# Change to a fused attention and mixture-of-experts kernel: expert weights by one-input products, second one-hots in columns over 32 steps, one late re-gather a step

## The chip, the core and the metric

One NeuronCore of a Trainium2 chip. The metric is the time of one execution in microseconds, as the device measures it; of several runs the median. Engines: TensorE (PE; its weight loads are PEld), VectorE (DVE), ScalarE (ACT), GpSimd (POOL) and SyncE (SP), which issues direct DMAs. Gathers and scatters by index are issued by GpSimd.

## The reference, cut to what matters

```python
# x, ctx: (64, 128, 256) f32
q = layernorm(x)
score = softmax(einsum('bci,bcj->bij', ctx, q) / 16, axis=0)    # over the 64 batches
x = x + einsum('bci,bij->bcj', ctx, score)
h = layernorm(x)                                                # 8192 tokens of 256
logits = h @ router_w.T                                         # 8 experts
top2, idx = top_k(logits, 2);  probs = softmax(top2)
y = sum over the 2 experts: probs * (gelu(h @ w1[e].T + b1[e]) @ w2[e].T + b2[e])
out = x + y
```

The softmax runs over the batches, so its maximum and its sum need all scores before any output. Each token goes to two of eight experts, so the tokens are sorted by expert.

## The kernel before

The work runs in stages, each a loop written once per engine; semaphores order the engines against each other.

1. Scores and their maximum over the batches, then the scores again with exponentials and their sum, both in 32 pairs of batches. The expert weights are transposed and split in two f16 parts beside the second pass.
2. `attend`, 32 pairs, software-pipelined: TensorE transposes ctx (L591), multiplies (L617), transposes the normalised rows (L599) and makes router logits (L607). GpSimd normalises the probabilities of the first 320 columns (L480) and works out the norm's scale (L452 to L457); VectorE normalises the other columns (L817), adds the residual (L781), takes statistics (L798, L813) and picks the top two. Eight weights a row (the softmax of the top two, spread over the experts) are written by L803, one product of two tensors for both batches of the pair. SyncE stores each pair's rows to a table in memory, 520 floats a token: the row so far, the normalised row in two f16 parts, the eight weights. Within `attend` the first 8 pairs and the tail are unrolled with fixed addresses, and 24 pairs run in a hardware loop.
3. Routing. Each token has a place in a list sorted by expert, for each of two rounds: in the first round it goes to the lower-numbered of its two experts, in the second to the other. `list_tokens` turns places into a list by TensorE: for each of the 64 batches a one-hot of the token's lane (128) is the weight and a one-hot of its tile (76), times a mark that holds the token's number, is the moving operand; 64 matmuls accumulate in one bank. VectorE makes the one-hots in `one_hots(rnd, q)`, 16 batches at a time, with the batch as the innermost, contiguous index, so TensorE reads them at a stride of 64 f16. `indices` turns the bank into gather and scatter indices.
4. Experts. Per round 38 groups of 256 tokens, 76 in all, in steps of one group, each step in the same order on each engine. In step i GpSimd gathers group i and then stores group i-4; TensorE does the first matmul of group i-3 (L664), the transposes of group i-2 (L675) and the second matmul of group i-4 (L687); ScalarE does the gelu (L1038) and copies the transposes (L1046); VectorE splits the activations of group i-3 in two f16 parts (L930, L932), adds its bias (L919), and adds the second matmul of group i-4 to the rows (L946). The first round reads the first table and writes the second; the second round reads the second table and writes the output.

At the boundary, groups 38 to 41 (the first four of round two) are gathered from the first table ahead of time, for the normalised rows alone; their running sums aren't known yet. In step 42 GpSimd waits for all stores of round one and then gathers these groups once more from the second table (L509, `late_loads`), and VectorE waits for that (`x_late_in`) before bias and sum of such a group. Each engine works through its instructions in order, so a wait holds all that is behind it.

The order: `one_hots(1, q)` stands in steps 0 to 3 behind the group's work on VectorE; `list_tokens(1)` at the end of step 36 on TensorE; `indices(1)` in step 37 on VectorE. Steps 0 to 5 are unrolled, 6 to 35 are a loop of six a turn, 36 to 47 are unrolled again.

Of the kernel before, what the change touches and what calls it, by code (L numbers as in the profile page):

```python
# [30 lines left out]
ALU = mybir.AluOpType  # L31
# [3 lines left out]
P = 128  # L35
BATCH, ROWS, DIM = 64, 128, 256
EXPERTS, HID = 8, 512
# [5 lines left out]
GROUPS = TOKENS // GROUP + EXPERTS - 2  # L43
TILES = GROUPS * SUB
# [6 lines left out]
PR = 2 * DIM  # L51
# [10 lines left out]
L_TR, L_G1, L_G2 = 2, 3, 4  # L62
# [74 lines left out]
def xattn_ffn(nc, x, ctx, router_w, w1, b1, w2, b2, out):  # L137
# [7 lines left out]
    with ExitStack() as stack:  # L145
# [31 lines left out]
        iota16 = smax[:, 0, 192:256].bitcast(F16)  # L177
# [3 lines left out]
        mark = smax[:, 0, 288:320].bitcast(F16)  # L181
# [18 lines left out]
        def slot(b, first, n):  # L200

            return slots[:, bass.ds(b * ROW + first, n)]

        def slot2(b, first, n):

            return slots3[:, bass.ds(b, 2), first:first + n]
# [143 lines left out]
        ALL = ROUNDS * GROUPS  # L350
        LIST_BANK = (4, 1)
        LIST_STEP = GROUPS // LANES * LANES

        def is_step(i, k, step):

# [2 lines left out]
        def is_late(g):  # L358

            return isinstance(g, int) and GROUPS <= g < GROUPS + L_G2  # L360

        def late_loads(step):

            first = step - L_G2 + (step > GROUPS + L_G2)
            return [g for g in range(first, step - L_G2 + 2) if is_late(g) and step >= GROUPS + L_G2]

        L_CTX = 2
        L_MAX = 3
# [163 lines left out]
        def _(pe):  # L532
# [104 lines left out]

            def list_tokens(rnd):

                tiles = tile_hot.rearrange("p (n b) -> p n b", b=BATCH)  # L640
                lanes = lane_hot.rearrange("p (l b) -> p l b", b=BATCH)
                w = BATCH // 4
                for b in range(BATCH):
                    q = b // w
                    if b % w == 0:
                        pe.wait_ge(r_lane, 4 * rnd + q + 1)
                        pe.wait_ge(r_tiles, 4 * rnd + q + 1)
                    mm = pe.matmul(psum[:, LIST_BANK[rnd], 0:TILES], lanes[:, :, b], tiles[:, :, b], start=(b == 0), stop=(b == BATCH - 1))
                mm.then_inc(r_list, 1)

            list_tokens(0)
# [45 lines left out]
        def _(dve):  # L697
# [63 lines left out]
            def attend(i, k, n):  # L761
# [38 lines left out]
                if live(i, k, L_P, PAIRS):  # L800
                    m, r2 = i + k - L_P, (k - L_P) % 2
                    dve.wait_ge(a_inv, m + 1)
                    dve.tensor_tensor(slot2(m * 2, PR, EXPERTS), exps[:, r2, :, 0, :], inv[:, r2, :].unsqueeze(2).to_broadcast([P, 2, EXPERTS]),  # L803
                                      ALU.mult).then_inc(a_comb, 1)
                if live(i, k, L_LG, PAIRS):
                    m, r2 = i + k - L_LG, (k - L_LG) % 2
                    dve.wait_ge(a_topi, m + 1)
# [67 lines left out]
            def one_hots(rnd, q):  # L875
# [8 lines left out]
                dve.wait_ge(r_ones, 4 * rnd + q + 1)  # L884
                dve.tensor_tensor(hot_b, one, mark[:, b].unsqueeze(1).to_broadcast([P, TILES, BATCH // 4]), ALU.mult).then_inc(r_tiles, 1)

            def indices(rnd):

                dve.wait_ge(r_list, rnd + 1)
                own = slice(rnd * TILES, (rnd + 1) * TILES)  # L890
                chain(dve.tensor_scalar(listed, psum[:, LIST_BANK[rnd], 0:TILES].bitcast(I32), 13, None, ALU.arith_shift_right))
                chain(dve.tensor_scalar(index_in[:, own], listed, float(-LISTED_ZERO), 0.0, ALU.add, ALU.max),
                      dve.tensor_scalar(empty, listed, 0.0, float(LISTED_ZERO + SKIPPED), ALU.is_equal, ALU.mult))
                dve.scalar_tensor_tensor(index_out[:, own], listed, float(-LISTED_ZERO), empty, ALU.add, ALU.add).then_inc(r_index, 1)
# [28 lines left out]
            def group(i, k, n, rnd):  # L923
# [23 lines left out]
                                                        rows[:, X2:X2 + DIM], ALU.mult, ALU.add)  # L947
                    last.then_inc(x_sum, 1)

                if isinstance(i, int) and i + k < 4:  # L950
                    one_hots(1, i + k)
                if is_step(i, k, LIST_STEP + 1):
                    indices(1)
            expert_steps(dve, group)
# [112 lines left out]
```

## Time and profile before

| | us |
|---|---|
| median of 3 runs | 801.28 (800.5 to 802.1) |
| profiled execution | 800.47 |
| its span on the core | 798.6 |

| engine | busy us | share of the span |
|---|---|---|
| TensorE matmul | 728.4 | 91% |
| TensorE weight load | 632.7 | 79% |
| VectorE | 620.0 | 78% |
| GpSimd | 538.7 | 67% |
| ScalarE | 384.9 | 48% |

The mean granted clock of TensorE was 0.949 of 2.4 GHz. A matmul's record lasts longer than its share of the engine, since they are pipelined; the spacing of starts is what it costs. A wait for a port or a lock counts as busy time of the instruction that waits, a wait for a semaphore as idle time ahead of it. Timelines give start, duration, engine, line, operation, count, and in brackets idle time before it with what ended it.

### The profile page before, as it was taken

What the parts mean: (1) busy time and instruction counts of PE and PEld (TensorE: products, weight loads), DVE (VectorE), ACT (ScalarE), POOL (GpSimd) and SP (SyncE); (2) the same over time, 40 slices, a digit from 0 to 9 for tenths busy, and PEclk for the clock granted to TensorE, in tenths of its full rate; (3) what the DMA queues carried; (4) which work ended last, traced back from release to release, by engine and by line L of the source; (5) the groups of instructions that cost most, each with busy time, mean ns of one, the idle gap of its engine ahead of it and who ended that gap; (6) DMA issues with size and microseconds to landing.
All of it is one profiled execution on the core that took longest, in us unless ns stands there. A gap on an engine that the chain in (4) does not pass through costs nothing. (4 is left out here: it accounts for less than half of the span.)

```text
span 798.6 us, 22383 instructions
## 1 busy us (share of the span) xinstructions
PE 728.4 (91%) x5819; PEld 632.7 (79%) x5820; DVE 620.0 (78%) x1514; ACT 384.9 (48%) x738; POOL 538.7 (67%) x649
## 2 busy tenths in 40 slices
PE   6999999599999955499999999999979999999995
PEld 4777888487777744399999999998967999999994
DVE  6998999989999988787777777636466777676764
ACT  3554666457777763144444444514433544444441
POOL 5664777678888840647777777754677777777753
PEclk9999999799999965699999999979999999999998
DMA  7887777247788751435555555653354444444440
GB/s 236 252 260 236 237 227 226 90 133 243 259 262 261 252 203 59 113 124 195 169 196 177 190 169 161 188 152 88 103 155 143 141 123 149 120 149 124 145 128 29
DMA packets 81630, 137.09 MB, mean 172 GB/s; under 512 B 9755, under 2 KB 54820, under 8 KB 81456
## 3 DMA queue, kind: packets, MB, share of 16 engines
q0 software_dynamic: 22528, 68.06, 28.1%
q1 hardware_dynamic: 59056, 68.46, 26.9%
q8 instruction: 24, 0.39, 0.2%
q14 instruction: 22, 0.18, 0.1%
HBM read 94.00 MB, written 47.24 MB: 177 GB/s over the span
## 5 line engine op out<-in xcount | busy, mean ns | idle before, releaser
L1038 ACT ACTIVATE work<-psum,b1T 128x256 f32<-128x256 f32 x304 | 127.7, 471 | 252.7 <-PE psum L664 250.1
L664 PE MATMUL psum<-work,w1T_high 128*128 128x256 f16 x1216 | 206.5, 275 | 2.8 <-ACT work L1046 2.8
L687 PE MATMUL psum<-w2T_high,slots 128*128 x1216 | 206.4, 275 | 0.9 <-issue 0.9
L664 PE MATMUL psum<-work,w1T_low 128*128 128x256 f16 x608 | 167.2, 275 | 0.0
L687 PE MATMUL psum<-w2T_low,slots 128*128 x608 | 167.2, 275 | 0.0
L664 PEld LDWEIGHTS psum<-work,w1T_high 128*128 x1216 | 119.9, 99 | 18.0 <-issue 3.3
L545 PE MATMUL psum<-slots,work 128*128 (+1 forms) x512 | 124.8, 392 | 7.0 <-ACT slots L963 5.8
L930 DVE CAST slots<-work 128x512 f16<-128x512 f32 x152 | 66.6, 438 | 81.9 <-ACT work L1038 80.5
L687 PEld LDWEIGHTS psum<-w2T_high,slots 128*128 128x128 f16 x1216 | 116.8, 99 | 14.5 <-issue 1.4
L518 POOL DMA_INDIRECT slots<-rows_first,slots x84 | 86.3, 1027 | 55.7 <-issue 53.5
L545 PEld LDWEIGHTS psum<-slots,work 128*128 128x128 f32 x512 | 93.7, 192 | 33.3 <-issue 17.7
L525 POOL DMA_INDIRECT rows_second<-slots x76 | 81.3, 1070 | 54.1 <-issue 29.7
L932 DVE TENSOR_TENSOR slots<-work,slots 128x512 f16<-128x512 f32 x152 | 106.4, 700 | 5.2
L525 POOL DMA_INDIRECT out_x<-slots x76 | 80.8, 1063 | 41.0 <-issue 34.3
L919 DVE SCALAR_TENSOR_TENSOR slots<-slots 128x256 f32<-128x256 f32 x152 | 67.4, 484 | 41.5 <-issue 28.1
L1046 ACT ACTIVATE work<-psum 128x1024 f16<-128x1024 f16 x76 | 77.8, 1024 | 28.3 <-PE psum L675 28.3
L518 POOL DMA_INDIRECT slots<-rows_second,slots x68 | 68.9, 1013 | 20.7 <-issue 20.7
L946 DVE SCALAR_TENSOR_TENSOR slots<-psum,slots 128x256 f32<-128x256 f32 x152 | 66.6, 479 | 19.0 <-DVE slots L919 11.7
L617 PE MATMUL psum<-slots,work 128*128 (+1 forms) x256 | 64.6, 396 | 4.5 <-DVE slots L817 4.5
L472 POOL TENSOR_TENSOR smax<-slots,smax 128x768 f32<-128x768 f32 x31 | 56.5, 1822 | 17.0 <-ACT slots L970 15.1
L664 PEld LDWEIGHTS psum<-work,w1T_low 128*128 x608 | 60.1, 99 | 7.4
L687 PEld LDWEIGHTS psum<-w2T_low,slots 128*128 128x128 f16 x608 | 60.0, 99 | 7.5
(124 smaller groups left out, 1092.4 us busy)
## 6 DMA issues: line engine op xcount, KB each, us to landing
work<-in_ctx SPq DMA_DIRECT2D x96, 256.0 KB, 3.4
rows_first<-slots SPq DMA_DIRECT2D x32, 520.0 KB, 3.1
slots<-in_x SPq DMA_DIRECT2D x32, 256.0 KB, 3.9
work<-in_L_ffn_w SPq DMA_DIRECT2D x32, 256.0 KB, 3.3
work<-in_x SPq DMA_DIRECT2D x32, 256.0 KB, 3.1
slots<-rows_first,slots POOLq DMA_INDIRECT x84, 3.6
rows_second<-slots POOLq DMA_INDIRECT x76
slots<-rows_second,slots POOLq DMA_INDIRECT x76, 3.6
```

The lines of the kernel that those rows point to most:

```text
L518: pool.indirect_dma_start(row_buf[r * SUB + s], None, source, bass.IndirectOffsetOnAxis(ap=index_in[:, g * SUB + s:g * SUB + s + 1], axis= ...
L525: pool.indirect_dma_start(table[1] if g < GROUPS else out_rows, bass.IndirectOffsetOnAxis(ap=index_out[:, g * SUB + s:g * SUB + s + 1], ax ...
L545: mm = pe.matmul(psum[:, r2, h * DIM:(h + 1) * DIM], ctx_ring[:, place, h * P:(h + 1) * P], slot(b, 0, DIM), start=True, stop=True)
L617: mm = pe.matmul(psum[:, 2 + r, j * DIM:(j + 1) * DIM], a_ctxT[:, 2 * r + j, h * P:(h + 1) * P], slot(m * 2 + j, h * DIM, DIM), start=(h = ...
L664: mm = pe.matmul(h, w1T[pw][:, f, c, bass.ds(e * P, P)], xT[r2][:, (px * HC + c) * GROUP:(px * HC + c + 1) * GROUP], start=(c == 0 and px ...
L687: mm = pe.matmul(y, act16[r2][pa][:, f * GROUP + s * P:f * GROUP + (s + 1) * P], w2T[pw][:, f, bass.ds(e * DIM, DIM)], start=(f == 0 and p ...
L919: last = dve.scalar_tensor_tensor(rows[:, X2:X2 + DIM], b2_all[:, bass.ds(e * DIM, DIM)], rows[:, bass.ds(e + PR, 1)], rows[:, X2:X2 + DIM ...
L930: dve.tensor_copy(act16[r2][0][:, cols], act32[r2][:, cols]).then_inc(x_high, 1)
L932: dve.tensor_tensor(act16[r2][1][:, cols], act32[r2][:, cols], act16[r2][0][:, cols], ALU.subtract).then_inc(x_low, 1)
L946: last = dve.scalar_tensor_tensor(rows[:, X2:X2 + DIM], psum[:, 6 + r2, s * DIM:(s + 1) * DIM], rows[:, bass.ds(e + PR, 1)], rows[:, X2:X2 ...
L1038: last = act.activation(act32[r2][:, f * GROUP:(f + 1) * GROUP], psum[:, 2 + 2 * r2 + f // 2, (f % 2) * GROUP:(f % 2 + 1) * GROUP], ACT.Ge ...
L1046: act.activation(xT[r2], psum[:, 0, :].bitcast(F16), ACT.Copy).then_inc(x_xT, 1)
```

## The change

Three parts. The expert weights of a pair are two `tensor_scalar` products, one a batch, whose scalar is the column `inv` read per partition, in place of one `tensor_tensor` over both. The one-hots of the second round are laid out with the batch outermost, made for two batches at a time in steps 4 to 35 (`LIST_FROM` is 36 - 32 = 4), and `list_tokens(1)` reads them as contiguous blocks behind one wait. `late_loads(step)` gives one group a step: 38 in step 42, 39 in 43, 40 in 44, 41 in 45, where it gave 38 and 39 in step 42, 40 in 43 and 41 in 44.

```diff
--- before.py
+++ after.py
@@ -350,6 +350,7 @@
         ALL = ROUNDS * GROUPS
         LIST_BANK = (4, 1)
         LIST_STEP = GROUPS // LANES * LANES
+        LIST_FROM = LIST_STEP - BATCH // 2
 
         def is_step(i, k, step):
 
@@ -361,8 +362,7 @@
 
         def late_loads(step):
 
-            first = step - L_G2 + (step > GROUPS + L_G2)
-            return [g for g in range(first, step - L_G2 + 2) if is_late(g) and step >= GROUPS + L_G2]
+            return [step - L_G2] if is_late(step - L_G2) else []
 
         L_CTX = 2
         L_MAX = 3
@@ -637,15 +637,18 @@
 
             def list_tokens(rnd):
 
-                tiles = tile_hot.rearrange("p (n b) -> p n b", b=BATCH)
-                lanes = lane_hot.rearrange("p (l b) -> p l b", b=BATCH)
-                w = BATCH // 4
                 for b in range(BATCH):
-                    q = b // w
-                    if b % w == 0:
-                        pe.wait_ge(r_lane, 4 * rnd + q + 1)
-                        pe.wait_ge(r_tiles, 4 * rnd + q + 1)
-                    mm = pe.matmul(psum[:, LIST_BANK[rnd], 0:TILES], lanes[:, :, b], tiles[:, :, b], start=(b == 0), stop=(b == BATCH - 1))
+                    if rnd:
+                        lane, tile = lane_hot[:, b * P:(b + 1) * P], tile_hot[:, b * TILES:(b + 1) * TILES]
+                        if b == 0:
+                            pe.wait_ge(r_lane, 4 + BATCH // 2)
+                            pe.wait_ge(r_tiles, 4 + BATCH // 2)
+                    else:
+                        lane, tile = lane_hot.rearrange("p (l b) -> p l b", b=BATCH)[:, :, b], tile_hot.rearrange("p (n b) -> p n b", b=BATCH)[:, :, b]
+                        if b % 16 == 0:
+                            pe.wait_ge(r_lane, b // 16 + 1)
+                            pe.wait_ge(r_tiles, b // 16 + 1)
+                    mm = pe.matmul(psum[:, LIST_BANK[rnd], 0:TILES], lane, tile, start=(b == 0), stop=(b == BATCH - 1))
                 mm.then_inc(r_list, 1)
 
             list_tokens(0)
@@ -800,8 +803,9 @@
                 if live(i, k, L_P, PAIRS):
                     m, r2 = i + k - L_P, (k - L_P) % 2
                     dve.wait_ge(a_inv, m + 1)
-                    dve.tensor_tensor(slot2(m * 2, PR, EXPERTS), exps[:, r2, :, 0, :], inv[:, r2, :].unsqueeze(2).to_broadcast([P, 2, EXPERTS]),
-                                      ALU.mult).then_inc(a_comb, 1)
+                    for j in range(2):
+                        last = dve.tensor_scalar(slot(m * 2 + j, PR, EXPERTS), exps[:, r2, j, 0, :], inv[:, r2, j:j + 1], None, ALU.mult)
+                    last.then_inc(a_comb, 1)
                 if live(i, k, L_LG, PAIRS):
                     m, r2 = i + k - L_LG, (k - L_LG) % 2
                     dve.wait_ge(a_topi, m + 1)
@@ -884,6 +888,19 @@
                 dve.wait_ge(r_ones, 4 * rnd + q + 1)
                 dve.tensor_tensor(hot_b, one, mark[:, b].unsqueeze(1).to_broadcast([P, TILES, BATCH // 4]), ALU.mult).then_inc(r_tiles, 1)
 
+            def one_hots_of_second(j):
+
+                b = BATCH + j * 2
+                one, two = tile_one[:, bass.ds(j * 2 * TILES, 2 * TILES)], tile_hot[:, bass.ds(j * 2 * TILES, 2 * TILES)]
+                as_tiles, as_lanes = "p (b n) -> p b n", "p (b l) -> p b l"
+                dve.tensor_tensor(one.rearrange(as_tiles, b=2), tile_of[:, bass.ds(b, 2)].unsqueeze(2).to_broadcast([P, 2, TILES]),
+                                  iota16[:, 0:TILES].unsqueeze(1).to_broadcast([P, 2, TILES]), ALU.is_equal).then_inc(r_ones, 1)
+                dve.tensor_tensor(lane_hot[:, bass.ds(j * 2 * P, 2 * P)].rearrange(as_lanes, b=2), lane_of[:, bass.ds(b, 2)].unsqueeze(2).to_broadcast([P, 2, P]),
+                                  iota16.unsqueeze(1).to_broadcast([P, 2, P]), ALU.is_equal).then_inc(r_lane, 1)
+                dve.wait_ge(r_ones, j + 5)
+                dve.tensor_tensor(two.rearrange(as_tiles, b=2), one.rearrange(as_tiles, b=2), mark[:, bass.ds(j * 2, 2)].unsqueeze(2).to_broadcast([P, 2, TILES]),
+                                  ALU.mult).then_inc(r_tiles, 1)
+
             def indices(rnd):
 
                 dve.wait_ge(r_list, rnd + 1)
@@ -947,8 +964,8 @@
                                                         rows[:, X2:X2 + DIM], ALU.mult, ALU.add)
                     last.then_inc(x_sum, 1)
 
-                if isinstance(i, int) and i + k < 4:
-                    one_hots(1, i + k)
+                if rnd == 0 or (isinstance(i, int) and LIST_FROM <= i + k < LIST_STEP):
+                    one_hots_of_second(i + k - LIST_FROM)
                 if is_step(i, k, LIST_STEP + 1):
                     indices(1)
             expert_steps(dve, group)
```

## Rows read from the trace of the kernel before

**Rows 1.** The page's first part: busy us (share) and instructions of each engine.
```profile
PE 728.4 (91%) x5819; PEld 632.7 (79%) x5820; DVE 620.0 (78%) x1514; ACT 384.9 (48%) x738; POOL 538.7 (67%) x649
```
**Rows 2.** Busy time by stretch; the last three columns are clock, DMA share, GB/s.
```profile
core 0: us, PE busy (x) PEld busy (x) DVE busy (x) ACT busy (x) POOL busy (x), PEclk, DMA share, GB/s
230.00:250.00 20.00, 18.57 (x120) 15.80 (x120) 20.00 (x88) 14.18 (x37) 16.57 (x25) 1.00 0.82 265
530.00:536.00 6.00, 6.00 (x39) 6.00 (x38) 0.00 (x0) 0.00 (x0) 2.88 (x3) 0.50 0.72 190
```
**Rows 3.** Timeline of VectorE in the loop of attend.
```profile
237.09 0.88 DVE L803 TENSOR_TENSOR slots<-smax 128x16 f32 x1
237.90 0.16 DVE L808 CAST smax<-topi 128x4 uint32 x1
237.97 0.24 DVE L813 BATCH_NORM_AGGREGATE mv<-stats 128x2 f32<-128x6 f32 x2
238.13 0.52 DVE L817 TENSOR_TENSOR slots<-slots,smax 128x384 f32 x1
```
**Rows 4.** Timeline of GpSimd in the same stretch.
```profile
236.41 1.54 POOL L480 TENSOR_TENSOR slots<-slots,smax 128x640 f32 x1
238.37 0.36 POOL L452 TENSOR_SCALAR veps<-mv 128x2 f32<-128x2 f32 x1 [0.42 <-DVE mv L813]
...
240.39 1.54 POOL L480 TENSOR_TENSOR slots<-slots,smax 128x640 f32 x1
```
**Rows 5.** Timeline of VectorE, two instructions with one input.
```profile
176.61 0.98 DVE L808 CAST smax<-topi 128x4 f32<-128x4 uint32 x1
...
289.68 4.24 DVE L770 TENSOR_SCALAR smax<-smax 128x2 f32<-128x2 f32 x1
```
**Rows 6.** Timeline of GpSimd at the same two places.
```profile
176.01 1.55 POOL L480 TENSOR_TENSOR slots<-slots,smax 128x640 f32<-128x640 f32 x1
...
289.33 4.56 POOL L493 IOTA slots<- 128x4864 f16 x1 [1.88 <-DMA rows_first<-slots]
```
**Rows 7.** Groups by line and form: count, busy us, mean ns, idle before.
```profile
L803 DVE TENSOR_TENSOR slots<-smax 128x16 f32 x24 | 22.5, 936 | 0.0
...
L842 DVE TENSOR_TENSOR slots<-slots,before 64x1024 f16<-64x1024 f16 x1 | 1.2, 1216 | 0.0
```
**Rows 8.** Waits between 400 and 523 us: total, times, longest.
```profile
DVE slots L930 <- ACT work L1038: 18.7, 35, 1.1
```
**Rows 9.** Timeline of TensorE: the second list, and the next transposes.
```profile
526.08 10.68 PE L648 MATMUL psum<-slots 128*128 128x76 f16 x64
540.90 0.61 PE L675 MATMUL psum<-ident,slots 128*128 128x128 f16 x8
```
**Rows 10.** The chain of work that ended last, at the boundary: start, us, what.
```profile
586.09 3.62 DMA slots<-rows_second,slots
...
601.38 4.46 PE psum L687 x24
605.84 2.62 PE psum L664 x24
608.46 0.45 PE psum L675 x8
608.90 2.62 PE psum L687 x24
```
**Rows 11.** Timeline of GpSimd at the boundary.
```profile
575.82 0.95 POOL L509 DMA_INDIRECT slots<-rows_second,slots  x1 [0.30 <-issue]
...
581.91 1.27 POOL L525 DMA_INDIRECT out_x<-slots  x1 [1.22 <-issue]
```
**Rows 12.** Timeline of VectorE at the boundary.
```profile
580.02 0.88 DVE L946 SCALAR_TENSOR_TENSOR slots<-psum,slots 128x256 f32<-128x256 f32 x2
...
591.64 0.88 DVE L946 SCALAR_TENSOR_TENSOR slots<-psum,slots 128x256 f32<-128x256 f32 x2
...
600.03 0.88 DVE L946 SCALAR_TENSOR_TENSOR slots<-psum,slots 128x256 f32<-128x256 f32 x2
...
602.34 0.69 DVE L932 TENSOR_TENSOR slots<-work,slots 128x512 f16<-128x512 f32 x1
```

## The prediction

> **What bounds the kernel now.** I read the page's shares first [rows 1]: TensorE is busy 91% of the 798.6 us span, VectorE 78%. An average over unlike stages says little, so next came the busy time by stretch [rows 2] and, for each place that the change touches, the timelines of the engines that meet there. The profiled execution took 800.47 us, its span plus 1.87 around it; the runs' median is 801.28, so what the sum gives is raised by 0.8 for the forecast. Differences under 0.2% (1.6 us) could not be told from no change.
>
> Attention: between 230 and 250 VectorE is busy all of the time and TensorE 18.57 of 20 [rows 2]. A pair of batches takes 3.98 us: the spacing of GpSimd's two products [rows 4]. The reader should see one thing in [rows 3, 4]: L803, 16 elements a partition, lasts 0.88 us and ends at 237.97, just when GpSimd's L480 (236.41 plus 1.54 = 237.95) lets go. In the 24 pairs of the loop it lasts 936 ns on average [rows 7]. It waits for GpSimd; the work is small.
>
> Experts: TensorE bounds. A group costs it 0.45 for transposes and twice 2.62 [rows 10], 5.69 us. Two things break that: the second token list, 64 matmuls in 10.68 us [rows 9], and the boundary of the rounds.
>
> **Part 1, the expert weights (L803).** One two-input product becomes two one-input products, each with a per-partition scalar from SBUF. If these didn't wait, VectorE would have 0.8 us less per pair. Do they wait? The trace has no such instruction, but two near it. The cast L808, one input, lasted 0.98 us at 176.61 [rows 5] and ended at 177.59, with GpSimd's L480 running from 176.01 to 177.56 [rows 6]; this was a pair in which L803 wasn't there yet. The tensor_scalar L770, two elements, lasted 4.24 us at 289.68 and ended at 293.92 [rows 5], with GpSimd's iota L493 from 289.33 to 293.89 [rows 6]. So a cast and a tensor_scalar wait for GpSimd as L803 does. The new instruction is a tensor_scalar of f32 in SBUF; what sets it apart is that its scalar is read from memory. I take it to wait.
>
> The Trainium skill speaks against this edit in the same way (SBUF — State Buffer, Who interferes with whom): copies, casts and tensor_scalars can enter a mode that takes both ports and so contend with GpSimd. The trace agrees with it in the two rows above. The same section says that a one-input instruction outside these modes doesn't contend; that would be rival A.
>
> Then the loop is this. L813 ends, GpSimd starts L452 at 238.37, its L480 ends at 241.93 [rows 4], L803 is let go, L808 and L813 follow, and GpSimd starts again. Everything between L480's end and L813's lies on the cycle. The second product adds one small instruction there: 0.07 us, the distance from L808 to L813 [rows 3]. Over 32 pairs: **+2.3 us** (0 to +3). This is also what VectorE pays where nothing waits.
>
> **Part 2, one-hots in columns, and the list.** Removed: 4 sets of three long instructions in steps 0 to 3. Three sets lay in the time before the first hidden block, where VectorE has nothing else, and the fourth after the first group's casts; TensorE waited there for gathers and for ScalarE's copy of the transposes, not for VectorE. Worth nothing. GpSimd's first gathers lose a neighbour, but the first of them is issued before these one-hots. Zero, at most -1.
>
> Moved to steps 4 to 35: three instructions of 152, 256 and 152 elements a step, each with an operand repeated along its innermost dimension. L842, f16 with such an operand, took 1216 ns for 1024 elements [rows 7], 1.19 ns each. 560 elements come to 0.66, and three starts at 0.07 [rows 3] make 0.87 us a step, as an upper end; with the fixed part of L842 left out, about 0.8. What covers it: between 400 and 523 VectorE waited 18.7 us for ScalarE's activations [rows 8], over 123/5.69 = 21.6 steps, 0.87 us a step. The cover is as large as the cost and not larger. Some lag can also be absorbed once: the last one-hots are due only behind TensorE's second block of the step after, so about one block of 2.62 us [rows 10]. So I cost it at **+0.3**. If loop addresses and extra waits add 0.2 us a step, 32 steps give 6.4, less 2.6: up to +4 (rival C). What queues behind these instructions is the next group's casts, and behind them TensorE's second matmul a step later.
>
> The list itself: before, weights and moving columns are read at a stride of 128 bytes; 10.68/64 = 167 ns a pair [rows 9]. After, both are contiguous. The nearest rows are the transposes L675, also a 128x128 f16 weight load and a matmul each, contiguous: 8 in 0.45 us, 56 ns each [rows 10]. 64 of them: 3.6 us. **-7.1**. Behind the list the granted clock was 0.50, of 2.4 GHz, which is the lower of its levels: it stood at that from 530 to 536 [rows 2] after sparse matmuls, and the following L664 block ran from 526.08 + 10.68 = 536.76 to 540.90 [rows 9], 4.14 us where 2.62 is the rule [rows 10]. A list of 3.6 us ends at 529.7, ahead of the first stretch that is at 0.50, so I take the clock to stay up: **-1.5**. Together -8.6. The other end: at half clock twice 56 ns, 7.2 us, and no clock gain: -3.5.
>
> The Trainium skill (TensorE: Matmul & The Clock Gate, Back-to-back issue gap) gives about 81 ns for a sustained pair of weight load and matmul of 128 columns. By that estimate the list takes 5.2 us and the forecast is 1.6 us higher. The trace shows 56, and the measurement decides.
>
> **Part 3, the late re-gathers.** Groups 38 to 41 must be gathered again from the second table. Before, GpSimd issues 38 and 39 in step 42, 40 in 43, 41 in 44: each but the first one step ahead. After, 38, 39, 40, 41 in steps 42, 43, 44, 45: the step in which VectorE needs them. On GpSimd's queue a re-gather stands behind the store of the group before, and that store waits for VectorE's sum of that group, which itself waited for its re-gather. So they become a chain. Its period can be read off, since before has one such link, from the sum of 38 to the sum of 40. The second half of the sum of 38 ends at 580.90 [rows 12]; store at 581.91 [rows 11]; the re-gather's second half issued at 586.09 lands 3.62 later [rows 10]; bias and sum end at 592.52 [rows 12]. 11.6 us. Before, it carried two groups, since 39 had been issued at 575.82 [rows 11]. After, each group needs one: sums of 39, 40, 41 at 592.5, 604.1, 615.8 on before's clock, where before has the last at 600.03 + 0.88 = 600.9 [rows 12].
>
> Who waits: VectorE works in order, so the casts of group 43 stand behind the sum of 41. Casts and differences end 603.03 - 600.91 = 2.1 us after it [rows 12], so at 617.9. TensorE needs them for its second matmul of group 43, which before started at 608.90 [rows 10]: 9.1 us later. It will have idled long by then, and after the idle at the same boundary such a block took 4.46 instead of 2.62 [rows 10]: 1.8 more. **+10.9** (+9 to +11.5). What is given back: the three gathers after that are issued behind one re-gather each instead of two at first, so the early part of the boundary's stall shrinks, but all of it lies before the new last wait. Afterwards GpSimd needs 4 issues of about 1.25 us [rows 11] in 5.69, so it doesn't fall behind. If a stall of this size were hidden, it would be through slack of VectorE to TensorE, some 3 to 4 us; that is already used in the recurrence.
>
> **Sum:** 800.47 + 2.3 + 0.3 - 8.6 + 10.9 = 805.4; with 0.8 up to the median, 806.2, stated as 806.0.
>
> **The rivals.** *A, the other side: the products don't wait for GpSimd* (27%). For: they read one tensor only. Against: [rows 5, 6]. Then L817, two inputs [rows 3], meets L480 in L803's place, so the 0.8 isn't all gained: GpSimd's own work from L452 to the end of L480 is 3.56 us [rows 4] and TensorE's 18.57 of 20 [rows 2] is 3.70 a pair. The period falls from 3.98 to 3.70, over 24 pairs -7, and the +2.3 goes: 796.7. It decides once the freed time is over 0.2 us a pair. *B, the late chain costs half* (8%), if VectorE's delay were taken up by the order of TensorE's work: 800.5. *C, VectorE becomes the bound of the first round* (10%): 810. *D, the contiguous list is no faster* (5%): the change doesn't do what it says there; 814.6.
>
> **Numbers.** Forecast 50%, at 806, itself 803 to 809. A 795 to 799.5, B 799 to 802. The range 795.5 to 809.5 leaves out the low edge of A, most of C, and D. Faster is nearly all of A and a little of B: 0.30; same, most of B: 0.08; slower, the forecast, C and D: 0.62.
>
> **What would show it.** Part 1: the last product ends with L480, its first lasting some 0.8 us, period 4.05; A shows both at 0.1 and L817 long, period 3.7. Part 2: list under 4 us at clock 1.00, the next L664 block 2.62; VectorE's wait for ScalarE near zero in steps 4 to 35, TensorE without gaps. Part 3: sums of 38 to 41 each 11.6 us apart and TensorE idle before group 43. I am wrong if [rows 5] don't speak for a scalar read from memory, or if that chain is shorter.

## The result, and the profile after

The changed kernel takes **810.17 us** (median of 4 runs, 809.6 to 811.9) where the kernel before took 800.93 on the same chip: ratio 1.0103, 95% interval 1.0086 to 1.0121, slower by 9.2 us (1.0%). Its profiled execution took 810.69 us with a span of 808.8, against 800.47 and 798.6 before.

First the page's first part: busy us, share of the span and instructions of each engine.

```profile
PE 726.9 (90%) x5819; PEld 629.5 (78%) x5820; DVE 635.4 (79%) x1630; ACT 384.9 (48%) x738; POOL 536.2 (66%) x649
```

Against [rows 1] TensorE has the same instructions, VectorE 116 more and 15.4 us more busy time. That says nothing of where 10.2 us of span went. For this, take the start of the same instruction in both profiled executions at a few places and see how the distance changes:

| place | before | after | after is late by | new in this stretch |
|---|---|---|---|---|
| routing's cast behind attention, VectorE | 301.50 | 308.83 | 7.33 | +7.33 |
| second token list, TensorE | 526.08 | 533.35 | 7.27 | -0.06 |
| first transposes behind it | 540.90 | 538.54 | -2.36 | -9.63 |
| sum of group 38, VectorE | 580.02 | 577.62 | -2.40 | -0.04 |
| second block of group 44, TensorE | 614.43 | 624.29 | 9.86 | +12.26 |
| end of the span | 798.6 | 808.8 | 10.2 | +0.3 |

One large gain, two large losses, and nothing in the 225 us of routing and round one. Now each of them in the timelines (start us, duration us, engine, line; brackets: idle before it, and what ended it). Line numbers are those of the changed kernel: its products are L807, its cast into `choice` L812, the list's matmuls L651, the two blocks' matmuls L667 and L690, the transposes L678, the bias L936, the sum L963, the casts L947, the differences L949; the second round's one-hots are L896, L898 and L901. L817 is the norm's statistics, for which GpSimd's L452 waits; L1055 is ScalarE's gelu.

VectorE and then GpSimd, in the loop of attention:

```profile
242.65 1.01 DVE L807 TENSOR_SCALAR slots<-smax 128x8 f32 x2
243.57 0.16 DVE L812 CAST smax<-topi 128x4 uint32 x1
243.64 0.23 DVE L817 BATCH_NORM_AGGREGATE mv<-stats 128x2 f32<-128x6 f32 x2
```

```profile
241.96 1.54 POOL L480 TENSOR_TENSOR slots<-slots,smax 128x640 f32 x1
244.04 0.36 POOL L452 TENSOR_SCALAR veps<-mv 128x2 f32<-128x2 f32 x1 [0.54 <-DVE mv L817]
246.06 1.55 POOL L480 TENSOR_TENSOR slots<-slots,smax 128x640 f32 x1
```

The two products together last 1.01 us and end at 243.66; GpSimd's L480 ended at 241.96 + 1.54 = 243.50. The first waits as the single one did in [rows 3, 4]. Only then comes the second, so GpSimd's L452 starts 0.54 behind its own L480, where it was 0.42, and the pair takes 246.06 - 241.96 = 4.10 us instead of 3.98.

TensorE at the list, and VectorE in a step of round one:

```profile
533.35 2.41 PE L651 MATMUL psum<-slots 128*128 128x76 f16 x64
535.91 0.39 PE L667 MATMUL psum<-work,w1T_high 128*128 128x256 f16 x2
```

```profile
404.81 0.31 DVE L896 TENSOR_TENSOR slots<-slots,smax 128x152 f16 x1
...
405.60 0.42 DVE L947 CAST slots<-work 128x512 f16<-128x512 f32 x1
```

The same 64 pairs of weight load and matmul, 2.41 us in place of 10.68 [rows 9], 38 ns each. The clock isn't what made the old list slow: its pairs started 164 ns apart in the first 3.7 us, at a granted clock of 1.00, and 165 ns apart in the rest, at 0.50. The block behind them runs from 535.91 to the transposes at 538.54, 2.63 us: full clock. The one-hots cost 405.60 - 404.81 = 0.79 us a step. Waits of VectorE between 400 and 523 us (total, times, longest) and the busy time in that stretch (PE, PEld, DVE, ACT, POOL, then clock, DMA share, GB/s):

```profile
DVE slots L947 <- ACT work L1055: 0.7, 4, 0.2
```

```profile
400.00:523.00 123.00, 123.00 (x1212) 111.19 (x1210) 103.19 (x238) 55.93 (x108) 90.45 (x88) 1.00 0.57 180
```

The wait for ScalarE, 18.7 us in [rows 8], is down to 0.7, and TensorE is busy all 123 us, as before. Group by group, its first blocks start 7.27 us later than before from group 1 to group 33, always the same distance: the one-hots went just where the slack was.

The boundary of the rounds. First the chain of work that ended last (start, us, what; L509 is the late re-gather, L525 the store), then TensorE's waits there, with the place in the profile before that the table's fifth row is measured from:

```profile
578.02 0.49 DVE slots L963
...
579.35 0.40 POOL out_x L525
...
580.75 1.00 POOL out_x L525
...
582.05 0.99 POOL slots L509
...
583.35 4.61 DMA slots<-rows_second,slots
...
589.25 0.49 DVE slots L936
...
590.28 0.49 DVE slots L963
...
616.52 4.06 PE psum L690 x24
```

```profile
580.76 0.39 PE L690 MATMUL psum<-w2T_high,slots 128*128 x2 [1.64 <-DVE slots L949]
590.02 1.03 PE L678 MATMUL psum<-ident,slots 128*128 128x128 f16 x8 [3.85 <-DMA slots<-rows_second,slots]
593.02 0.61 PE L690 MATMUL psum<-w2T_high,slots 128*128 x2 [1.96 <-DVE slots L949]
...
614.66 0.62 PE L678 MATMUL psum<-ident,slots 128*128 128x128 f16 x8 [2.61 <-DMA slots<-rows_second,slots]
616.52 0.61 PE L690 MATMUL psum<-w2T_high,slots 128*128 x2 [1.25 <-DVE slots L949]
...
624.29 0.39 PE L690 MATMUL psum<-w2T_high,slots 128*128 x2 [0.46 <-DVE slots L949]
```

```profile
614.43 0.38 PE L687 MATMUL psum<-w2T_high,slots 128*128 x2
```

Read the chain as a circle: sum, two stores, two re-gathers, landing, bias, sum. It goes round three times, from the sum of group 38 to that of 41. VectorE's four sums start at 577.62, 589.88, 601.83 and 613.38, that is 12.3, 12.0 and 11.5 us apart. TensorE now waits twice a turn: for gathered rows, and for L949, the differences that stand behind the late sum on VectorE.

### The profile page after: what moved, and what is told of

It is laid out like the page before. It is cut to its first block and busy times, and to the rows that moved or that the text cites. A ratio compares the mean times of both kernels' runs of the same rounds, so it can differ in the third digit from the quotient of the medians.

```text
span 808.8 us, 22700 instructions
## 1 busy us (share of the span) xinstructions
PE 726.9 (90%) x5819; PEld 629.5 (78%) x5820; DVE 635.4 (79%) x1630; ACT 384.9 (48%) x738; POOL 536.2 (66%) x649
## 5 line engine op out<-in xcount | busy, mean ns | idle before, releaser
L1055 ACT ACTIVATE work<-psum,b1T 128x256 f32<-128x256 f32 x304 | 127.5, 470 | 253.0 <-PE psum L667 250.3
L690 PE MATMUL psum<-w2T_high,slots 128*128 x1216 | 208.6, 277 | 7.2 <-DVE slots L949 7.1
L667 PE MATMUL psum<-work,w1T_high 128*128 128x256 f16 x1216 | 205.2, 274 | 3.0 <-ACT work L1063 2.8
L690 PE MATMUL psum<-w2T_low,slots 128*128 x608 | 168.5, 277 | 0.0
L667 PE MATMUL psum<-work,w1T_low 128*128 128x256 f16 x608 | 166.6, 274 | 0.0
L690 PEld LDWEIGHTS psum<-w2T_high,slots 128*128 128x128 f16 x1216 | 117.4, 99 | 22.2 <-issue 8.4
L667 PEld LDWEIGHTS psum<-work,w1T_high 128*128 x1216 | 119.4, 98 | 18.0 <-issue 3.6
L545 PE MATMUL psum<-slots,work 128*128 (+1 forms) x512 | 125.1, 393 | 7.0 <-ACT slots L980 5.9
L525 POOL DMA_INDIRECT out_x<-slots x76 | 80.3, 1057 | 54.6 <-issue 42.7
L936 DVE SCALAR_TENSOR_TENSOR slots<-slots 128x256 f32<-128x256 f32 x152 | 67.4, 484 | 58.3 <-issue 36.0
L525 POOL DMA_INDIRECT rows_second<-slots x76 | 80.2, 1056 | 46.3 <-issue 29.6
L947 DVE CAST slots<-work 128x512 f16<-128x512 f32 x152 | 67.7, 445 | 54.8 <-ACT work L1055 52.8
L949 DVE TENSOR_TENSOR slots<-work,slots 128x512 f16<-128x512 f32 x152 | 106.5, 701 | 5.2
L963 DVE SCALAR_TENSOR_TENSOR slots<-psum,slots 128x256 f32<-128x256 f32 x152 | 66.6, 479 | 19.8 <-DVE slots L936 14.2
L617 PE MATMUL psum<-slots,work 128*128 (+1 forms) x256 | 66.5, 406 | 4.5 <-DVE slots L821 4.5
L690 PEld LDWEIGHTS psum<-w2T_low,slots 128*128 128x128 f16 x608 | 60.3, 99 | 7.8
L667 PEld LDWEIGHTS psum<-work,w1T_low 128*128 x608 | 59.8, 98 | 7.3
```

What stands on the lines that cost most here:

```text
L525: pool.indirect_dma_start(table[1] if g < GROUPS else out_rows, bass.IndirectOffsetOnAxis(ap=index_out[:, g * SUB + s:g * SUB + s + 1], ax ...
L545: mm = pe.matmul(psum[:, r2, h * DIM:(h + 1) * DIM], ctx_ring[:, place, h * P:(h + 1) * P], slot(b, 0, DIM), start=True, stop=True)
L617: mm = pe.matmul(psum[:, 2 + r, j * DIM:(j + 1) * DIM], a_ctxT[:, 2 * r + j, h * P:(h + 1) * P], slot(m * 2 + j, h * DIM, DIM), start=(h = ...
L667: mm = pe.matmul(h, w1T[pw][:, f, c, bass.ds(e * P, P)], xT[r2][:, (px * HC + c) * GROUP:(px * HC + c + 1) * GROUP], start=(c == 0 and px ...
L690: mm = pe.matmul(y, act16[r2][pa][:, f * GROUP + s * P:f * GROUP + (s + 1) * P], w2T[pw][:, f, bass.ds(e * DIM, DIM)], start=(f == 0 and p ...
L936: last = dve.scalar_tensor_tensor(rows[:, X2:X2 + DIM], b2_all[:, bass.ds(e * DIM, DIM)], rows[:, bass.ds(e + PR, 1)], rows[:, X2:X2 + DIM ...
```

## The experiments

All are the kernel before with one edit, unless said otherwise. Each was timed beside runs of the kernel before on its own chip, whose medians were 801.4, 802.1 and 802.3 us, so the ratios and the differences in us are against those. They tell apart: does each part cost what its term of the sum says, do the parts add, and is the wait of the products really what sets attention's pace.

**One part alone.** The diffs are the three parts of the change. Part 1:

```diff
-dve.tensor_tensor(slot2(m * 2, PR, EXPERTS), exps[:, r2, :, 0, :], inv[...].to_broadcast(...), ALU.mult)
+for j in range(2):
+    last = dve.tensor_scalar(slot(m * 2 + j, PR, EXPERTS), exps[:, r2, j, 0, :], inv[:, r2, j:j + 1], None, ALU.mult)
```

> The kernel before with part 1 alone: two one-input products a pair in place of L803. Theory (the products wait for GpSimd's L480, and the second one adds its start): in the changed kernel the pair's period is 4.10 us against 3.98, so 24 pairs give 3 us and the unrolled ones 1 more: 4 us slower, 805. In the changed kernel's profile attention had lost 7.3 us, of which 3.6 lie in one place at 188 to 203 us where a ctx load took 5.5 us and TensorE's clock fell; if that belongs to the products, this kernel is 7 us slower, 808; if it is a chance of that execution, it is absent here. Rival (they don't wait and the loss is elsewhere): faster, or the same.

Measured: 805.82 us, ratio 1.0053 (1.0032 to 1.0074), +4.4 us. GpSimd's L480 recurs every 4.10 us and, once a turn of the loop, 4.34 (before 3.98 and 4.20); its eighth and its last start are 99.68 us apart, against 96.76 before: +2.9 in 24 pairs. VectorE's row is that of the whole change, its rows moved in time only:

```profile
239.42 1.01 DVE L804 TENSOR_SCALAR slots<-smax 128x8 f32 x2
```

Part 2 is the one-hots in columns and the contiguous list (the diff's `one_hots_of_second` and `list_tokens`):

> The kernel before with part 2 alone: the second round's one-hots in columns over steps 4 to 35, and the contiguous list. Theory: in the changed kernel the first round took 194.18 us from its first L664 block to the list against 194.06, and from the list to the next transposes 5.19 against 14.82, so 9.6 us faster, 791, if the boundary moves as a whole with it. Rival (the boundary is bound by GpSimd, which was given time by the long list): half of it is taken back at the boundary, 796.

Measured: 790.79 us, ratio 0.9868 (0.9851 to 0.9885), -10.6 us. TensorE at the list:

```profile
526.28 2.41 PE L652 MATMUL psum<-slots 128*128 128x76 f16 x64
```

It starts 0.2 us later than before (routing's cast is 0.27 later too), so round one lost nothing, and the next transposes come at 531.40, 9.50 earlier. The other 1.2 us of the profile came at the boundary. The block of group 42, 4.46 us in [rows 10], took 2.79 here: TensorE's granted clock between 590 and 600 was 1.00, where before had 0.83 from 600 to 610. But that isn't part 2's doing. The same block in the chains of two runs told below, which gather late as before: first with the product moved ahead, where the list is the old one, then the whole without part 3, where it is the new one:

```profile
600.15 2.79 PE psum L687 x24
...
597.84 4.46 PE psum L691 x24
```

Either length occurs with either list, so this 1.2 us is a difference between executions, and what part 2 gains by its trace is the 9.50, inside the 9.2 to 11.9 of the runs.

Part 3, one late re-gather per step:

```diff
-first = step - L_G2 + (step > GROUPS + L_G2)
-return [g for g in range(first, step - L_G2 + 2) if is_late(g) and step >= GROUPS + L_G2]
+return [step - L_G2] if is_late(step - L_G2) else []
```

> The kernel before with part 3 alone: one late re-gather a step. Theory (a chain of 11.6 to 12 us from sum to sum): sums of 38 to 41 stand 11.6 to 12 us apart, the second block of group 43 starts about 10 us later, 11 to 12 us slower, 812. Rival (part of the loss in the changed kernel comes of part 2, whose short list leaves GpSimd or VectorE no pause before the boundary): 5 to 8 us slower, 807.

Measured: 815.27 us, ratio 1.0173 (1.0156 to 1.0190), +13.9 us. The sums are 11.9, 11.5 and 12.1 us apart. The chain shows the same circle (lines are one less than the unchanged code's, L508 the re-gather, L524 the store):

```profile
584.02 1.00 POOL out_x L524
...
585.33 0.99 POOL slots L508
...
586.62 4.29 DMA slots<-rows_second,slots
```

The expectation had 11 to 12 us; the median shows 13.9 (12.5 to 15.2), the trace of this run, whose time was the lowest of its four, 12.1 at the boundary. Each part has the sign that the sum gave it, and 4.4 - 10.6 + 13.9 = +7.7 beside the whole's 9.2; the intervals reach about 1.5 us to either side of each part, so this is agreement. The whole without part 3 asks the same from the other side:

> The changed kernel with the late chain taken back (products and one-hots as in the change, the late re-gathers as before). Additive parts: 801.4 + 4.4 - 10.6 = 795.2 us (before x 0.9922), and the late chain then costs 810.2 - 795.2 = 15 us in the company of the other two, against the 13.9 that it cost alone. Rival: the parts share a cost (the list's early end gives the late chain a head start, or a longer attention hides part of it): the late chain then costs clearly less than 13.9 here and this kernel runs at 797 us or more.

Measured: 796.58 us, ratio 0.9922 (0.9901 to 0.9944), -5.7 us where parts 1 and 2 alone sum to -6.2. The late chain in company costs (1.0103 - 0.9922) x 801 = 14.5 us, beside 13.9 alone. The parts add, within these intervals; by the traces they lie in separate stretches.

**Does the kind of product matter?** A single product over both batches, with a constant as its scalar. This leaves out the division by the row's own sum, so it is for the timing alone:

```diff
-dve.tensor_tensor(slot2(m * 2, PR, EXPERTS), exps[:, r2, :, 0, :], inv[...].to_broadcast(...), ALU.mult)
+dve.tensor_scalar(slot2(m * 2, PR, EXPERTS), exps[:, r2, :, 0, :], 0.0078125, None, ALU.mult)
```

> The kernel before with L803 as a single one-input product over both batches, its scalar an instruction constant and not the row's own factor; so the expert weights aren't divided by their own sum, which leaves out that part of the computation. Theory (a one-input product waits for L480 as the two-input one does, whatever its scalar, and the loss of the products is only the second instruction): it lasts about 0.88 us in the loop, the period is 3.98, the time is that of the kernel before, 801. Rival (the products wait only because their scalar is read from memory): it lasts 0.2, and the cast behind it waits 0.65 as in the run with L803 moved; 799.

Measured: 801.27 us, ratio 0.9988 (0.9971 to 1.0005): nothing. VectorE's row, with GpSimd's L480 from 236.56 to 238.10:

```profile
237.25 0.89 DVE L803 TENSOR_SCALAR slots<-smax 128x16 f32 x1
```

It ends at 238.14, with L480 again, and the period is 3.98. A product with one input waits for GpSimd whether its scalar comes from memory or not. What part 1 lost comes of the second product and, it seems, of the memory scalar too. Where GpSimd isn't at work (part 1 alone, then this run):

```profile
284.98 0.35 DVE L804 TENSOR_SCALAR slots<-smax 128x8 f32<-128x8 f32 x2
285.24 0.16 DVE L809 CAST smax<-topi 128x4 f32<-128x4 uint32 x1
...
281.41 0.15 DVE L803 TENSOR_SCALAR slots<-smax 128x16 f32<-128x16 f32 x1
281.48 0.16 DVE L807 CAST smax<-topi 128x4 f32<-128x4 uint32 x1
```

The cast starts 0.26 us behind the pair and 0.07 behind the single product with a constant, 0.13 for each product with a memory scalar in place of 0.07. Two products with constants weren't run, so how much of it each of the two differences makes is not shown.

**Can the wait be avoided?** The product as it was, moved in VectorE's order ahead of `max_index`, where L480 hasn't begun:

```diff
+(L803's product, here)
 for j in range(2):
     last = dve.max_index(topi[:, r2, j, :], ...)
 ...
-(L803's product, from here)
```

> The kernel before with L803 unchanged in kind but moved ahead of max_index, to where GpSimd is in its short steps and L480 hasn't begun. Theory (L803 waits for L480 by its place, and in its absence L817 meets the end of L480): L803 lasts about 0.15 us, L817 gets longer than 0.52, the pair's period falls from 3.98 to 3.6 to 3.7, GpSimd's own work or TensorE's; 24 pairs give 7 us, 794. Rival (the period is set by something else, such as the ctx loads): L803 short, the period stays near 3.98, the same time.

Measured: 799.02 us, ratio 0.9972 (0.9958 to 0.9985), -2.3 us. VectorE's and GpSimd's timelines:

```profile
236.78 0.17 DVE L794 TENSOR_TENSOR slots<-smax 128x16 f32 x1
...
237.81 0.65 DVE L810 CAST smax<-topi 128x4 uint32 x1
...
236.88 1.55 POOL L480 TENSOR_TENSOR slots<-slots,smax 128x640 f32 x1
238.77 0.36 POOL L452 TENSOR_SCALAR veps<-mv 128x2 f32<-128x2 f32 x1 [0.34 <-DVE mv L815]
```

The product is down to 0.17 us, but the cast behind it, 4 elements with one input, now lasts 0.65 and ends at 238.46, L480 at 238.43. The wait has moved to the next instruction that meets L480; only 0.08 us, about what one small instruction takes, left the cycle, and the period is 3.90, not the 3.6 to 3.7 expected. So the cast was moved too, to the end of VectorE's step:

> The kernel before with L803 ahead of max_index and the cast L808 at the end of the pair's work, so that neither stands beside L480. In the run with L803 alone moved, the cast took 0.65 us, again to the end of L480, and the period was 3.90. Theory (the next instruction that can wait does): now only L817 waits, behind L813, so GpSimd is no longer held by VectorE's wait; the period falls to 3.6 to 3.7 and the kernel to 793 or 794. Rival (another chain, such as ScalarE's copies or the ctx loads, binds at 3.85): 798.

Measured: 802.98 us, ratio 1.0006 (0.9995 to 1.0016): the gain of the move before is gone, and the 793 or 794 expected was missed. The steady period is 3.76, as short as hoped, but once in every turn of the loop it is 5.15. There GpSimd is ahead, its L480 starts at 249.40 and the early product of the next pair is caught:

```profile
249.40 1.54 POOL L480 TENSOR_TENSOR slots<-slots,smax 128x640 f32 x1 [0.18 <-issue]
252.41 0.44 POOL L452 TENSOR_SCALAR veps<-mv 128x2 f32<-128x2 f32 x1 [1.48 <-DVE mv L811]
...
249.45 1.52 DVE L794 TENSOR_TENSOR slots<-smax 128x16 f32 x1
```

1.52 us of waiting in front of all of VectorE's step, and GpSimd in turn idle 1.48. A turn of four pairs takes 3.76 + 3.76 + 3.94 + 5.15 = 16.6 us, where before it took 16.15; over 24 pairs 98.39 in place of 96.76. With VectorE's order as it was, every pair pays a little; with this one, one pair in four pays much.

**How much cover was there in round one?** Part 2 alone, with two more one-hot instructions of 256 and 152 elements a step, into buffers that nobody reads any more:

```diff
+dve.tensor_tensor(lane_no[...two batches...], lane_of[...].to_broadcast([P, 2, P]), iota16..., ALU.is_equal)
+dve.tensor_tensor(tile_no[...two batches...], tile_of[...].to_broadcast([P, 2, TILES]), iota16..., ALU.is_equal)
```

> Part 2 alone, with two more one-hot instructions (256 and 152 elements) in each of the steps 4 to 35, written where nobody reads: 0.56 us more of VectorE a step. Theory (part 2's 0.77 us a step fill VectorE's 0.87 of cover, so more of it comes out): 32 steps by 0.56 are 18 us, less 0.1 a step of cover left and some 3 us of lag that can be absorbed: 10 to 15 us slower than part 2 alone, 803. Rival (VectorE's other gaps close as well, so there is more cover than the waits for ScalarE): under 5 us slower than part 2 alone, 795.

Measured: 801.14 us, ratio 0.9989 (0.9975 to 1.0003), some 10 us above part 2 alone. The one-hots now cost 444.90 - 443.55 = 1.35 us a step, and TensorE has gaps:

```profile
443.55 0.31 DVE L896 TENSOR_TENSOR slots<-slots,smax 128x152 f16 x1
...
444.90 0.42 DVE L951 CAST slots<-work 128x512 f16<-128x512 f32 x1
...
400.00:523.00 123.00, 118.73 (x1140) 104.15 (x1139) 106.31 (x266) 53.15 (x102) 88.87 (x82) 1.00 0.53 169
```

The list starts 10.1 us later than in part 2 alone. TensorE's first blocks tell where: their distance to part 2 alone stays at 0.94 us from group 1 to group 12 and then grows to 10.1 at group 34. So the first steps lose nothing, which I take to be lag that is absorbed once, and the other 22 lose 9.2 us, 0.42 each. 1.35 - 0.42 = 0.93 us a step can be hidden for good, near the 0.87 of [rows 8]; the change used 0.79. The edge is real and the change stops short of it by some 0.14 us a step.

**Is it the order on GpSimd's queue?** The kernel before, with the step's ordinary gather issued ahead of the late re-gathers (except that of group 38):

```diff
-for g in late_loads(i): (late re-gathers)
+for g in [g for g in late_loads(i) if g == GROUPS]: (late re-gather of 38)
 (the step's gather)
+for g in [g for g in late_loads(i) if g != GROUPS]: (the others)
```

> The kernel before with GpSimd's gather of the step's group ahead of the late re-gather (but for group 38, which stays first). Theory (at the boundary TensorE waits three times for an ordinary gather, 2.89, 0.85 and 1.71 us, each queued behind late re-gathers on GpSimd): these waits go, VectorE's sums of 40 and 41 come 2.5 us later, which TensorE doesn't feel, and its clock stays up; 3 to 5 us faster, 797. Rival (the sums are what TensorE waits for next): within 1 us of before, 801.

Measured: 803.00 us, ratio 1.0015 (1.0001 to 1.0029). The 3 to 5 us that were expected didn't come. In the trace the transposes behind the list are 3.5 us later than before, which lies ahead of the edit, and group 44's second block is 3.1 later. The boundary itself changed by -0.4 us, within what two executions differ by. TensorE's first two waits there are 0.54 us (for rows) and 1.28 (for VectorE's differences) in place of 2.89 and 0.33, but the sums of groups 40 and 41 come 3.1 us later, counted from the list, and with them the stores and gathers behind them on GpSimd, for which TensorE then waits in small pieces. The stall is only dealt out differently. The chain that ended last runs through a turn of store, re-gather and sum in either order, which I take to be what sets the end; that part is argued from two traces and not tested.

**The version without the losing parts.** Part 2, alone again as a neighbour on the same chip, and part 2 with the product moved ahead:

> The kernel before with only the second round's one-hots in columns, the same program as e2_columns, run again so that the two kernels below stand beside it on one chip. Every theory: 790 to 791.5 us, ratio to before 0.985 to 0.989.

> The one-hots in columns (as e2_columns) and, in attention, the product of the expert weights moved ahead of the two index searches in the step, where e4_early had a period of 3.90 against 3.98 us and -2.3 us in all. If the two gains lie in separate stages, as the traces say (attention ends before the list begins), they add: 790.8 - 2.3 = 788.5 us, ratio 0.983 to 0.985 to before and 0.996 to 0.998 to e13_columns_again. Rival: the earlier end of attention only lengthens the wait of the first gathers and nothing reaches the end: 790.8 us.

Measured: 791.36 us, ratio 0.9862 (0.9837 to 0.9888), and **788.73 us**, ratio 0.9831 (0.9808 to 0.9854), 2.6 us below its neighbour. Both gains reach the end, and this version beats the kernel before by 13.6 us and the changed one by some 21 (by the two ratios, since those two ran on different chips).

## Why the prediction was right, and where its terms were off

The forecast was 806, the result 810.2. The direction and the mechanisms of all three parts are those that the sum was made of, but the number was not close. It lies outside the 803 to 809 of the forecast itself and 0.7 us above the top of the whole range, 809.5; only the ratio puts it on that edge (801.28 x 1.0103 = 809.5). It is also the 810 of rival C, whose mechanism isn't in the trace. And the sum was helped by luck: against the runs of the parts the products were put 2.1 us too low and the late chain 3.0, while the list was put 2.0 too high and the one-hots 0.3. Together that is 2.8 us; another 1.5 are what the whole is above its parts. Term by term:

- **The products wait (+2.3 forecast).** They do. Forecast was +0.07 a pair, from the distance between two small instructions in [rows 3]. Measured +0.12 in the loop (0.54 for 0.42 ahead of L452), and alone the part cost 4.4 us. The row was the wrong one: L808 to L813 is the start-to-start distance of two other small instructions, and these products take 0.13 each where they don't wait. 24 pairs give +2.9; behind the loop, where GpSimd's other instructions are, part 1 alone lost another 1.75 in its profiled execution (from L480's last start in the loop to routing's cast 26.58 us for 24.83), but the whole only 0.56, so of that some is spread between executions. With the 0.26 for 0.07 of the rows above, the seven pairs of the tail would give 7 x 0.19 = 1.3 and the whole 4.2, an estimate, near the 4.4. The rule cited from the Trainium skill (SBUF — State Buffer, Who interferes with whom) held wherever it could be seen: tensor_scalars of 8 and 16 elements and the cast of 4 ended with L480. A trace shows that wait, not the mode that they ran in.
- **Attention in the profiled execution lost 7.3, not 2.3.** Of this 0.3 us were there at attention's first transposes, 0.1 came before the loop, 6.3 in its 24 pairs and 0.6 behind them. Of the 6.3, 2.9 is the second product (as in part 1 alone), and 3.4 is one stall, seen in the starts of L480 on GpSimd and in two rows of TensorE:

```profile
192.72 1.54 POOL L480 TENSOR_TENSOR slots<-slots,smax 128x640 f32 x1
198.94 1.54 POOL L480 TENSOR_TENSOR slots<-slots,smax 128x640 f32 x1
204.60 1.54 POOL L480 TENSOR_TENSOR slots<-slots,smax 128x640 f32 x1 [0.18 <-issue]
...
188.07 0.66 PE L591 MATMUL psum<-ident,work 128*128 128x128 f32 x4 [2.56 <-DMA work<-in_ctx]
190.50 3.76 PE L617 MATMUL psum<-slots,work 128*128 x8
```

  TensorE waited 2.56 us for a context load, and its next matmuls, 3.76 us where they take 1.97 elsewhere, ran at half clock. Part 1 alone and the whole without part 3 have the same attention code and go without the stall (24 pairs in 99.7 and 99.8 us), though they wait for the load at the same place, 1.56 and 2.46 us, at full clock. And two runs with the attention code of before do have a smaller one: part 2 again, and the reordered gathers, wait 1.83 and 1.99 us there, fall to half clock, and take 98.0 us for their 24 pairs in place of 96.8. The first of them:

```profile
188.01 0.66 PE L592 MATMUL psum<-ident,work 128*128 128x128 f32 x4 [1.83 <-DMA work<-in_ctx]
...
189.75 3.37 PE L618 MATMUL psum<-slots,work 128*128 x8
```

  So the stall doesn't need the products. But all three traces with part 1 have a wait of over 1.5 us there, and only two of the other ten; whether part 1 makes it likelier stays open. The profiled execution lies in the middle of the kernel's runs, which are 1.5 us above the sum of the three parts.
- **The one-hots are covered (+0.3).** Measured -0.06 in the whole and 0 alone. The cost, 0.79 us a step, was the "about 0.8" of the estimate, and the cover, 0.93 by the run with more one-hots, was close to the 0.87 of [rows 8]. Rival C fell, but by 0.14 us a step only.
- **The list (-8.6).** -9.6 in the profile of the whole, -10.6 alone. The list's time was the mis-sized term, 2.41 us and not 3.6: the transposes in [rows 10] move 128 columns a pair, the list 76, and 38 ns for 76 columns is nearer to the ratio of the columns (56 x 76/128 = 33) than to the same price; from start to start it is 35. I took the row over without scaling it. The clock's share was -1.36 for -1.5. The estimate by the Trainium skill (TensorE: Matmul & The Clock Gate, Back-to-back issue gap), from about 81 ns for a sustained pair at 128 columns, was 5.2 us. The 56 ns of [rows 10] are below that figure, the row was nearer, and the truth lay beyond the row. Rival D fell.
- **The late chain (+10.9).** +12.3 in the whole's profile, and 13.9 and 14.5 by the medians. The circle and who waits for it were right. The turn was 11.5 to 12.3 us, not 11.6 each time: landing took 4.61 us in the first turn for the 3.62 of the row. That made group 43's second block 10.2 later and not 9.1 (the list's share taken off). From there to group 44's it took 7.77 us for 5.69, 2.1 more and not 1.8: the block itself took 4.06 in place of 2.62, 1.4 more, and the rest is mostly group 44's wait of 0.46 for L949. Note that the 4.46 that the 1.8 was read from is itself a length that comes and goes between executions, as seen above. TensorE's waits are also seen in its clock, the third column from the right:

```profile
580.00:600.00 20.00, 13.43 (x95) 10.61 (x96) 4.43 (x9) 3.09 (x6) 11.45 (x12) 0.74 0.37 105
600.00:620.00 20.00, 12.97 (x96) 9.78 (x95) 11.79 (x26) 5.40 (x10) 10.03 (x10) 0.83 0.31 95
```

  Rival B, that half of it would be hidden, fell. Between the 12.3 of the trace (12.1 in that of part 3 alone) and the 14 of the medians some 2 us aren't placed; the intervals reach 1.4 us to either side.
- **Rival A** fell twice over. Its condition fell (the products wait), and its arithmetic too: it held that with L803 out of the way the period would be 3.70. With L803 really out of the way it was 3.90, since the cast took the wait over, and with both out 3.76 and a lost loop turn. I had looked for the next waiting instruction among those with two inputs (L817) and passed over L808, which stands in [rows 5] as one that waits.

## What to carry to other kernels

When an instruction is long because it waits for another engine, changing its kind or splitting it doesn't shorten it; look for the place in the order where the other engine isn't at work, and then ask which instruction meets that engine next. A transfer issued one step early may be the one thing that keeps store, gather and use from becoming a circle: count the turn of the circle before making the issue "just in time". Before a stretch of one trace is credited to an edit, look for the same stretch in runs that don't have the edit. And of three edits that come together, price and time each by itself, since here one of them, worth 1.3%, was buried under the two others.

## What the runs showed of the hardware

- The layout made 64 pairs of weight load and matmul 4.4 times faster: 10.68 us with weights and columns read at a stride of 128 bytes, 2.41 us with both contiguous. I had expected a factor of 3. The strided pairs were as slow at a granted clock of 1.00 (164 ns) as at 0.50 (165 ns). Which of the two strides costs the time was not tested.
- A one-input product of 16 elements with a constant scalar lasted 0.89 us, with a scalar from memory (twice 8 elements) 1.01, and a cast of 4 elements 0.65, each ending within 0.2 us of GpSimd's product. The shortest of the 32 products with a constant, clear of that neighbour, took 0.15; the products with a scalar from memory took 0.20 or more each.
- A short wait of TensorE can cost more than itself: before, a wait of 1.71 us was followed by a block of 4.46 us in place of 2.62 [rows 10]; in part 2 alone the same block took 2.79 after a wait of 1.69, at full clock. Both lengths occur in executions with the same boundary code; what decides between them was not shown.
